# Two transformer layers on one core: norms in halves, gates folded into weights, a changed order around the triangular inversions

## The reference, cut to what matters

```python
h = _layernorm(x) * (1 + ca) + sa
x = x + ga * attention0(h)            # 16 heads of 8, causal softmax, then @ w_proj
h = _layernorm(x) * (1 + cb) + sb
x = x + gb * experts(h)               # 8 experts, 2 per token, out = relu(h W1 + b1) W2 + b2
# second layer, with its own sa, ca, ga, sb, cb, gb
h = _layernorm(x) * (1 + ca) + sa
x = x + ga * gated_delta_net(h)       # 12 heads, keys of 64, values of 128
h = _layernorm(x) * (1 + cb) + sb
x = x + gb * ffn(h)
```

```python
S = S * exp(g_t);  delta = (v_t - k_t S) * b_t;  S = S + k_t delta;  o_t = q_t S
o = o * rsqrt(mean(o*o)) ;  o = o * silu(h @ Wg) ;  out = o @ Wo
```

## Time and profile before

| | us |
|---|---|
| median of 3 runs | 2719.34 (2716.93 to 2723.6) |
| the profiled execution | 2734.56 |
| its span, first to last instruction | 2732.8 |
| TensorE busy | 2433.6 (89%) |
| VectorE busy | 1794.9 (66%) |
| ScalarE busy | 1455.4 (53%) |
| GpSimd busy | 825.4 (30%) |

### The profile page before, as it was taken

The page is one execution under the profiler, slowest core; times in us unless marked ns, Lnnn a source line. Parts: engine busy times, 40 slices in busy tenths (PEclk is TensorE's granted clock), DMA queues, the critical chain, the costliest instruction groups (busy, mean ns, idle before and its releaser), DMA issues.

```text
span 2732.8 us, 65917 instructions
## 1 busy us (share of the span) xinstructions
PE 2433.6 (89%) x24299; PEld 1680.0 (61%) x24299; DVE 1794.9 (66%) x4697; ACT 1455.4 (53%) x3129; POOL 825.4 (30%) x581
## 2 busy tenths in 40 slices
PE   3899988899898998989989899899988999889998
PEld 2456765477554775547745577456764567655676
...
DMA packets 226985, 138.31 MB, mean 51 GB/s; under 512 B 173567, under 2 KB 209799, under 8 KB 219431
## 3 DMA queue, kind: packets, MB, share of 16 engines
q1 hardware_dynamic: 208870, 125.48, 16.2%
...
...
## 4 chain that ended last, share of the span: by engine, by line
PE 50%; DVE 18%; ACT 15%; issue 8%; DMA 6%; SPq 2%; POOL 2%; ACTq 0%; DVEq 0%; POOLq 0%
PE bank L914 7%; PE bank L699 4%; PE bank L509 4%; PE bank L690 3%; DVE small L1367 3%; PE bank L1013 3%; PE bank L622 3%; ACT arena L1638 3%; ACT arena L1637 2%; PE bank L952 2%; DVE blk_tx L1369 2%; ACT vq L1645 2%; PE bank L547 2%; DVE mx L1171 2%; PE bank L602 2%
## 5 line engine op out<-in xcount | busy, mean ns | idle before, releaser
L1925 POOL TENSOR_TENSOR arena<-upto,gk 128x1536 f32<-128x1536 f32 x32 | 88.1, 2754 | 682.8 <-DVE beta L1308 682.8
L1315 DVE SCALAR_TENSOR_TENSOR arena<-bank,conv,arena 128x510 f32<-128x510 f32 x320 | 237.1, 747 | 45.1 <-ACT arena L1638 26.1
L509 PE MATMUL bank<-mask_k,ident_bf 128*128 128x512 bf16 x976 | 250.8, 391 | 0.0
L1171 DVE TENSOR_REDUCE mx<-bank 128x2 f32<-128x768 f32 (+3 forms) x187 | 201.5, 1123 | 47.2 <-PE bank L548 46.1
L1917 POOL TENSOR_TENSOR arena<-arena 128x511 f32<-128x511 f32 x160 | 201.8, 1272 | 56.8 <-DVE arena L1315 56.8
L1601 ACT ACTIVATE arena<-bank 128x384 f32<-128x384 f32 (+1 forms) x384 | 168.5, 544 | 49.3 <-PE bank L607 49.2
L760 PE MATMUL bank<-h_pad,arena 128*128 128x512 f32 x320 | 165.6, 615 | 28.7 <-DVE arena L1315 21.8
L547 PE MATMUL bank<-vq 128*128 128x512 bf16 (+3 forms) x544 | 123.2, 313 | 55.3 <-issue 32.9
L1367 DVE TENSOR_TENSOR small<-blk_tx,blk 96x1 f32<-96x1 f32 (+14 forms) x480 | 142.8, 297 | 16.5
L1622 ACT ACTIVATE arena<-bank,b1e 128x512 f32<-128x512 f32 x128 | 87.8, 686 | 116.8 <-PE bank L690 111.6
L1276 DVE SCALAR_TENSOR_TENSOR arena<-bank,comb,arena 128x128 f32<-128x128 f32 x256 | 72.0, 344 | 114.9 <-PE bank L699 113.7
...
## 6 DMA issues: line engine op xcount, KB each, us to landing
...
```

Of the source, the lines that this page charges most:

```text
L509: mm(PS[bank][:, :], ident_bf[:, :], mask_k[:, :, :].rearrange("p h w -> p (h w)"), start=True, stop=True)
L1171: V.reduce_max(dst, unit_scores(u), AX.X).then_inc(s_max, 1)
L1315: ins = V.scalar_tensor_tensor(a[:, k:T], ps[:, 0:T - k], conv[:, n, 3 - k:4 - k], a[:, k:T], ALU.mult, ALU.add)
```

## The change

Four things are done. **Norms in halves:** VectorE signals after two of the four normalised tiles, TensorE transposes two tiles into one bank and two into another, and `modulate` is two instructions of 256 columns. The fillers are 19 and 18 instead of 22 and 24 ahead of norms 1 and 2, and 2 instead of 4 behind. **Gates in weights:** once per pass GpSimd multiplies `w_proj`, the experts' second weights (2048 columns, after their DMA) and `b2` by the gates; VectorE's multiplications L1226 and L1280 and the separate sum L1282 go, since the experts' results are added to `xs` directly. **First chunk:** with a state of zero `key_part(0)`, `query_part(0)`, `differences(0)`, ScalarE's `query_part(0)` and `decay_state(0)` go; `unknowns(0)` reads the values themselves, and VectorE copies where it added. **Order:** `levels(3)` starts right behind `turn_out(1)`; the gate groups 1 and 2 of chunks 0 and 1, all three of chunk 2, and `project(1)` in two lots, now stand between the steps of the `levels` behind them, in place of fillers.

```diff
-        pe_stages += [("levels", 0), ("keys", 2), ("queries", 2), ("key_part", 0), ("mask", 2), ("unknowns", 0), ("query_part", 0),
-                      ("outputs", 0), ("gate_first", 0), ("gram", 2), ("attend", 2), ("gate", 0)]
+        pe_stages += [("levels", 0), ("unknowns", 0), ("keys", 2), ("queries", 2), ("outputs", 0), ("mask", 2),
+                      ("gate_first", 0), ("gram", 2), ("attend", 2)]
-                      ("outputs", 1), ("turn_out", 0), ("gram", 3), ("project", 0), ("attend", 3), ("gate_first", 1), ("gate", 1)]
+                      ("outputs", 1), ("turn_out", 0), ("gram", 3), ("project", 0), ("attend", 3), ("gate_first", 1)]
-                      ("outputs", 2), ("turn_out", 1), ("gate_first", 2), ("project", 1), ("gate", 2)]
-        pe_stages += [("levels", 3), ("enter_norm", 1), ("gate_first", 3), ("gate", 3), ("enter_qkv", 1),
+                      ("outputs", 2), ("turn_out", 1)]
+        pe_stages += [("levels", 3), ("enter_norm", 1), ("gate", 3), ("enter_qkv", 1),
-        act_stages += [("levels", 0), ("keys", 2), ("queries", 2), ("mask", 2),
-                       ("unknowns", 0), ("key_scale", 2), ("query_scale", 2), ("query_part", 0)]
+        act_stages += [("levels", 0), ("unknowns", 0), ("keys", 2), ("queries", 2), ("mask", 2), ("key_scale", 2), ("query_scale", 2)]
-        act_stages += [("gate", 1), ("rms", 1), ("levels", 2), ("query_part", 2), ("unknowns", 2), ("project", 1)]
-        act_stages += [("gate", 2), ("levels", 3), ("rms", 2), ("enter_norm", 1), ("enter_h", 1), ("gate", 3),
+        act_stages += [("levels", 2), ("rms", 1), ("gate", 1), ("query_part", 2), ("unknowns", 2), ("project", 1)]
+        act_stages += [("levels", 3), ("rms", 2), ("gate", 2), ("gate", 3),
-                       ("outputs", 1), ("gram", 3), ("project", 0), ("attend", 3), ("rms", 1)]
-        dve_stages += [("levels", 2), ("subst", 3), ("differences", 2), ("scale", 1), ("outputs", 2), ("project", 1)]
+                       ("outputs", 1), ("gram", 3), ("attend", 3)]
+        dve_stages += [("levels", 2), ("project", 0), ("rms", 1), ("subst", 3), ("differences", 2), ("scale", 1), ("outputs", 2)]
...
-                    bank, n = {1: (7, 22), 2: (5, 24), LEAVE: (7, 2)}[k]
+                    bank, n = {1: (7, 19), 2: (5, 18), LEAVE: (7, 2)}[k]
...
                     for s in range(8):
-                        keep_warm(3, {3: 4, 4: 2, 6: 2}.get(s, 0))
+                        if c < 2:
+                            if c and s in (1, 3):
+                                gate_group(0, 1 if s == 1 else 2)
+                            keep_warm(3, {3: 2 if c else 4, 4: 2, 6: 2}.get(s, 0))
+                        elif c == 2 and s in (3, 4):
+                            keep_warm(3, {3: 1, 4: 0}[s])
+                            gate_group(1, s - 2)
+                        elif c == 3 and s in (1, 3):
+                            project(1, range(0, 4) if s == 1 else range(4, HD))
+                        elif c == 3 and s in (4, 6, 7):
+                            gate_group(2, (4, 6, 7).index(s))
...
                     for g in range(NG):
-                        pe.wait_ge(r_ready, at(b, r_ready, NG * c + g + 1))
+                        if c:
+                            pe.wait_ge(r_ready, at(b, r_ready, NG * (c - 1) + g + 1))
...
+                            known = rb[:, h, :] if c else v_all[:, 0, h, :]
+                            last = mm(ps[:, j * P:(j + 1) * P], xw[:, h, :], known, start=True, stop=True)
...
             def modulate(b, k, dst, mod):
-                dve.wait_ge(ln_ps, at(b, ln_ps, k + 1))
-                V.tensor_scalar(dst, ln_bank[:, :], mod[:, 1:2], mod[:, 0:1], ALU.mult, ALU.add).then_inc(h_ready, 1)
+                for i in range(2):
+                    half = slice(T // 2 * i, T // 2 * (i + 1))
+                    dve.wait_ge(ln_ps, at(b, ln_ps, 2 * k + i + 1))
+                    V.tensor_scalar(dst[:, half], ln_banks(k)[i][:, half], mod[:, 1:2], mod[:, 0:1], ALU.mult, ALU.add).then_inc(h_ready, 1)
...
-                V.tensor_tensor(wide_t, tiles(proj_bank), gate_row(0), ALU.mult).then_inc(dve_step, 1)
-                dve.wait_ge(dve_step, step())
-                V.tensor_tensor(xs[:, :, :], xin[:, :, :], wide_t, ALU.add).then_inc(xin_free, 1)
+                V.tensor_tensor(xs[:, :, :], tiles(proj_bank), xin[:, :, :], ALU.add).then_inc(xin_free, 1)
...
-                V.tensor_tensor(moe, moe, gate_row(1), ALU.mult).then_inc(dve_step, 1)
-                dve.wait_ge(dve_step, step())
-                V.tensor_tensor(xs[:, :, :], xs[:, :, :], moe, ALU.add).then_inc(dve_step, 1)
...
+                G.tensor_tensor(wproj_g[:, :], wproj[:, :], gates[:, 0, :], ALU.mult).then_inc(wp_gated, 1)
+                G.tensor_tensor(w2t, w2t, gates[:, 1, :].unsqueeze(1).to_broadcast([P, NE * HT, D]), ALU.mult).then_inc(w2_gated, 1)
```

166 lines of the change are left out of this document (92 added, 74 removed).

## The result

| | before | changed |
|---|---|---|
| median | 2721.47 us (2716.93 to 2728.04, 4 runs) | 2766.40 us (2750.86 to 2770.14, 4 runs) |
| profiled execution | 2734.56 | 2750.86 |
| its span | 2732.8 | 2749.1 |
| granted clock, seven passes | 0.98 | 0.96 |

The ratio is 1.0148, 95% interval [1.0116, 1.0180]: some 45 us more in the medians, 5.6 us for each of the eight passes. The forecast was 2723, its upper end 2748. They show where the time goes, but not all of it.

The account below looks back on a forecast made before the run. The prediction took waits between engines, not TensorE's busy share, as the bound. Terms of -1.05 us a pass plus 1.5 for the clock made +0.45, +3.6 in all: 2723 us, range 2697 to 2748.

Parts of the forecast that it names:

- Norms: Norms 1, 2 and `LEAVE`: halves, gated weights and fewer fillers save 0.8, 2.1 and 0.4 us a pass.
- Hidden multiplication: GpSimd's gating of weights ahead of norm 1: taken as 3.7 us long, hidden, at a cost of 0.
- Chunk 0, +1.4: Behind `levels(0)`: late decays delay VectorE's copies of state and outputs, so `gram(2)` starts 1.4 us later.
- `levels(1)`, +1.7: In `levels(1)`: a gate group ahead of step 1, and step 3's group, Silu and table load, add 1.7 us a pass.
- `key_part(2)`: Behind `levels(2)`: TensorE idles some 3.9 us for ScalarE's Silu; +1.0 us, using up a start 1.2 earlier.
- `levels(3)`, -0.85: From `levels(3)` to L1563: it starts 5.2 us earlier but holds more work, so only 0.85 us a pass remains.
- Sum of -1.05, -8.4 in eight: Whole pass, without the clock's term: the waits and lengths together save 1.05 us a pass, 8.4 in eight.
- The clock, +1.5: State products behind `levels(2)`: a new clock fall costs 0 to 4.4 us a pass; a third taken, +1.5.
- rival C: TensorE's clock falls at chunk 2's state products in all passes, in chunk 0 in some: 2734 to 2758 us; chance 0.33.
- The signs: Wrong if TensorE doesn't wait at `gram(2)` and `key_part(2)`, or its clock at chunk 2's state products falls in no more passes.
- Rival B: TensorE's work is the bound, all removed work counts, 11.1 us a pass: 2630 us, with half 2675; chance 0.10.

Follow-up runs that it names:

- e5: e1 plus the first chunk without the products of the zero state, decays of chunk 2 ahead of the unknowns, gate groups as before: 2684 us, ratio 0.9830.
- e6: e5 with the change's own order in chunk 0, unknowns and outputs first and the decays of chunk 2 behind them: 2733 us, ratio 1.0014.
- e7: e5 with gate groups 1 and 2 of chunk 0 moved into `levels(1)`, ahead of steps 1 and 3, with two fillers less: 2699 us, ratio 0.9888.
- e8: e5 plus the change's order around `levels(3)`, begun right behind `turn_out(1)` with `project(1)` and chunk 2's gate groups inside: 2678 us, ratio 0.9820.
- e4: Changed kernel with the old order at `levels(2)`: chunk 1's gate groups and Silu ahead of it, fillers in their place: 2733 us, ratio 1.0010.
- e1: Kernel before with only the norms in halves, their fewer fillers, and the gates folded into weights: 2689 us, ratio 0.9847.
- e12: e1 with 27 fillers instead of 18 ahead of norm 2: 2729 us, ratio 0.9980.
- e13: e12 with more fillers in `levels(0)` to `levels(2)`, 5 ahead of step 1 and 3 ahead of steps 4 and 6: 2712 us, ratio 0.9899.
- e14: e1 with more fillers in `levels(0)` to `levels(2)`, 5 ahead of step 1 and 3 ahead of steps 4 and 6: 2728 us, ratio 0.9970.
- e11: e8 with more fillers in `levels(0)` to `levels(2)`, 5 ahead of step 1 and 3 ahead of steps 4 and 6: 2679 us, ratio 0.9794.

## Why the prediction was wrong, step by step

- **Norms.** Right. Norm 2's transposes -1.9, `levels(0)` -2.5 (-2.1 worked out); from the projection to the router's products the shortest pass is 6.65 us for 7.83 in norm 1 (-1.2; -0.8 worked out; the medians are 6.7 and 8.9). The fillers ahead of norm 1 in the earlier trace rows ran in part at 1.2 GHz: 0.27 us each there, 0.22 in the changed kernel's norm 2. Hidden multiplication: right.
- **Chunk 0, +1.4.** The place and the mechanism were right (VectorE's copies behind `key_scale(2)`, behind the late decays), the size only at full clock. I placed `gram(2)` 17.6 us behind `levels(0)`; it came at 17.4 and 17.5 in two passes, and at 19.0 in the three, the one shown among them, where the clock fell during the unknowns. From `levels(0)` to `levels(1)` it is +3.3. And the term compared with before alone; e5 and e6 show that the order threw away 50 us, 6 a pass, by itself.
- **`levels(1)`, +1.7.** +3.7: 16.2 us for 12.5. In the three passes without a fall in it `levels(1)` takes 14.9 us, +2.4, which is also how much later step 3's reads begin, directly behind the Silu and its table load as expected; the falls that begin at 153 or 154 us of the other four passes are the remainder. e7 puts the groups by themselves at 15 us in eight passes, near the 1.7.
- **`key_part(2)`.** The wait was forecast to 0.1 us (3.9 and 3.94). Its fall of the clock is in all seven passes.
- **`levels(3)`, -0.85.** Right in the mean: from the end of `levels(1)` to the successor of L1563, where the term ends, the mean is 79.5 us for 80.5 (the medians are 80.0 and 80.1), with the falls behind `levels(2)` inside it; -6 us in e8.
- **Sum of -1.05, -8.4 in eight.** Near. The table of differences leaves -11 us for the changed kernel against before once the clock is taken out, an estimate; the profiled executions (2339.06 us for seven passes against 2317.39, 3.1 a pass more, with 14.6 us more at 1.2 GHz) give 3.1 - 0.43 x 14.6 = -3.2 a pass. Both have the sign.
- **The clock, +1.5.** This is the step that failed. It was 0.43 x 14.6 = 6.3 us a pass by the slope of the prediction, and 52 us in all by the slope and the executions of the experiments. I took a third of one fall, with 4.4 as the upper end, for one place, since the falls of before stood there. There were four: the unknowns of chunk 0, `gram(2)`, `levels(1)` and `key_part(2)`, and the first three, which had none before and for which the sum has nothing, brought 10.3 of the 14.6 us. The rival C named the mechanism and one price too low: 2734 to 2758 against 2766.
- **The signs.** Both waits came, and the clock behind `levels(2)` is lower in more passes, so nothing that the prediction named as a sign of being wrong has shown: the signs tested the waits, which were right, and not the price of the clock.
- **Rival B** counted 13 fillers fewer at the norms. By the code it is 15, since the four behind the transposes became two at each of three norms; with the 17 of `levels` that makes the 32 a pass by which the pages' counts differ (976 and 720 in eight). Nothing in the forecast hangs on it.

The rule of the Trainium skill that I weighed against the change ("TensorE: Matmul & The Clock Gate", "HAM oscillation — how this bites in real kernels"), that gaps bring TensorE's clock down, is borne out at `key_part(2)`: the granted clock is 0.59 to 0.79 in seven windows of seven with the wait, 1.00 in five of seven without (e4). The drain behind a table load ("ScalarE: Activation LUTs", "What ACT_TABLE_LOAD costs") is not seen in the trace here either: 1277.20 plus 1.28, and the next instruction begins at 1278.50.

What stays open is what decides, between kernels without such waits, which inversion falls. e1, e12, e13 and e14 differ in fillers alone and lie up to 36 us apart. So the 41 us of the norms' part are shown as a measurement, but only some 20 of them as its own shorter waits. Why the clock falls in `levels(1)` in five passes of e5 and in none of e1 is open too.

Some versions beat both kernels: e1, e5, e8 and e11 are at 0.985, 0.983, 0.982 and 0.979. Their intervals all overlap; e8 keeps the change's norms, gated weights, first chunk and early `levels(3)`, and gives up its late decays, its gate groups in `levels(1)` and `levels(2)` and the Silu behind `levels(2)`.
